# A convolution and a routed-attention block on one core: a lag of four steps, loads in smaller pieces, softmax sums by a shuffle, and the two halves of the TensorE array used for score products side by side

## The reference, cut to what matters

```python
q_reg, k_reg = qr.mean(2), kr.mean(2)
_, idx = jax.lax.top_k(jnp.einsum('brc,bsc->brs', q_reg, k_reg), TOPK)        # TOPK = 4, 49 regions
kg = take(kr, idx)     # 4 regions x 64 keys for each region's 64 queries
vg = take(vr, idx)
scores = jnp.einsum('brqhd,brkhd->brhqk', qh, kh) * scale                     # 8 heads, d = 8
attn = jax.nn.softmax(scores, axis=-1)
out = jnp.einsum('brhqk,brkhd->brqhd', attn, vh)
x = x + out @ wo + bo
x = x + gelu(layernorm(x) @ w1 + bm1) @ w2 + bm2
```

## Time and profile before

| | |
|---|---|
| median of 3 runs | 5555.56 us (5546.46 to 5559.63) |
| the profiled execution | 5569.85 us, span 5568.0 us |
| mean granted TensorE clock | 0.909 of full speed |
| TensorE busy | 4677.0 us, 84% of the span |
| VectorE, ScalarE, GpSimd busy | 62%, 59%, 49% |
| moved by the DMA queues | 487.33 MB, 88 GB/s on the mean |

### The profile page before, as it was taken

How to read it: one execution, slowest core, us unless ns; L and a number is a source line. 1 busy time by engine, 2 the same in 40 slices (tenths; PEclk the granted TensorE clock), 3 DMA queues, 4 the chain that set the end, 5 groups by cost and what they waited for, 6 DMA issues and landing times.

```text
span 5568.0 us, 230234 instructions
## 1 busy us (share of the span) xinstructions
PE 4677.0 (84%) x68754; PEld 3217.0 (58%) x68754; DVE 3447.6 (62%) x7969; ACT 3285.4 (59%) x6282; POOL 2747.0 (49%) x9656
## 2 busy tenths in 40 slices
PE   2388888888889888888888888888888888888888
PEld 1265565656556565565656656565565656556564
DVE  2266666666666666666666666666566666667665
ACT  1156556565665656556565665656556565665656
POOL 1245455454544545445454554545455454554553
PEclk8589999998998999889989999989899999989999
DMA  1333343333333333333333423333343333323311
GB/s 53 102 98 92 83 109 76 100 77 96 102 77 98 84 95 91 82 103 80 94 83 91 111 72 103 81 96 92 79 109 79 96 81 102 100 75 102 84 40 33
DMA packets 627124, 487.33 MB, mean 88 GB/s; under 512 B 483792, under 2 KB 613968, under 8 KB 615536
## 3 DMA queue, kind: packets, MB, share of 16 engines
q10 hardware_dynamic: 335360, 205.62, 16.4%
q1 hardware_dynamic: 290416, 265.73, 16.2%
HBM read 262.38 MB, written 208.73 MB: 85 GB/s over the span
## 4 chain that ended last, share of the span: by engine, by line
PE 45%; DMA 18%; issue 10%; SPq 7%; ACT 7%; DVE 5%; DVEq 3%; POOL 2%; ACTq 2%; POOLq 1%
DMA max_d<-tr 11%; PE ps L988 9%; PE ps L1002 7%; PE ps L1019 7%; PE ps L881 4%; DMA qm<-qk_d 3%; PE ps L938 3%; DMA xin<-in_x 3%; DVEq L223 2%; DVE mx L724 2%; SPq L327 2%; PE ps L949 2%; PE ps L901 2%; ACT hid L813 2%; PE ps L974 2%
## 5 line engine op out<-in xcount | busy, mean ns | idle before, releaser
L724 DVE TENSOR_REDUCE mx<-ps 128x4 f32<-128x1024 f32 x1568 | 1921.7, 1226 | 1702.3 <-PE ps L988 1354.0
L832 ACT ACTIVATE pt<-ps 128x512 f32<-128x512 f32 x3136 | 1694.3, 592 | 869.2 <-PE ps L1002 814.4
L506 POOL COPY vg<-vs 64x64 f32 x6272 | 1526.5, 243 | 782.0 <-POOL kg L490 576.7
L988 PE MATMUL ps<-kg,qm 96*128 96x256 f32 x6272 | 1336.2, 338 | 386.6 <-DVE mx L724 127.3
L490 POOL CAST kg<-ks 96x128 fp32r x3136 | 851.0, 297 | 1511.6 <-PE ps L1002 1156.6
L988 PEld LDWEIGHTS ps<-kg,qm 96*128 96x128 f32 x6272 | 946.8, 202 | 1053.6 <-issue 889.5
L1002 PE MATMUL ps<-qm,kg 97*128 97x256 f32 x6272 | 1119.8, 301 | 178.8 <-ACT pt L832 102.3
L1019 PE MATMUL ps<-pt,vg 128*32 128x64 f32 x50176 | 1091.4, 231 | 0.0
L1002 PEld LDWEIGHTS ps<-qm,kg 97*128 97x128 f32 x6272 | 926.2, 203 | 252.2 <-ACT pt L832 164.8
L1019 PEld LDWEIGHTS ps<-pt,vg 128*32 128x32 f32 x50176 | 826.1, 115 | 224.2 <-issue 34.8
L643 DVE CAST kg<-ks 96x128 fp32r x3136 | 625.6, 241 | 126.2 <-issue 123.5
(11 more groups left out here) (109 smaller groups left out, 3866.7 us busy)
## 6 DMA issues: line engine op xcount, KB each, us to landing
qk_d<-stg SPq DMA_DIRECT2D x224, 448.0 KB
qm<-qk_d ACTq DMA_DIRECT2D x1792, 42.0 KB
ks<-qk_d ACTq DMA_DIRECT2D x96, 784.0 KB, 6.2
vs<-v_d ACTq DMA_DIRECT2D x64, 784.0 KB, 6.7
xin<-in_x SPq DMA_DIRECT2D x119, 224.0 KB
xi_d<-xi SPq DMA_DIRECT2D x112, 224.0 KB
qk_d<-stg SPq DMA_DIRECT2D x112, 224.0 KB
max_d<-tr SPq DMA_DIRECT2D x1568, 2.0 KB
```

The lines of the kernel that those rows point to most:

```text
L506: j = pool.tensor_copy(dst.rearrange("p j (e x) -> p j e x", e=2)[:, :, :, 0:HD], vs[place(m)[0]][rows, bass.ds(region, 1), :].rearrange(" ...
L724: v.tensor_reduce(mx[h % 2][:].rearrange("p (g j e) -> p g j e", g=2, j=2)[:, :, :, 0], ps[:, 0:2, :].rearrange("p g (j k) -> p g j k", j= ...
L832: act.activation(pt[m % 2][:, c], ps[:, 2 + c, :], ACT.Exp, scale=float(HD) ** -0.5).then_inc(S["pt_ready"], 1)
L988: i = pe.matmul(ps[:, g, 256 * j:256 * j + 256], qm[c % 2][0:NP3, t, g, 2 * j:2 * j + 2, :].rearrange("p h t -> p (h t)"), kg[slot][0:NP3, ...
```

## The change

- **Lag.** `turned` and `attended` run four and five steps behind `scores`; the timetables of preparation, finish and routing shift by one step. SP issues the hop of step h first and then the row of step h-2. The rings `mx`, `tr`, `hopped` have 7 places, and the reduce waits for no hop.
- **Loads.** Keys and values of an image come in 20 transfers, spread over 23 steps (first image) and 34 steps (second), in place of 5 over 10. Queries go out as 4 and 4 transfers, in the steps with h mod 7 = 4 and 5. Input strips are worked every 7 steps, over 6 steps each.
- **Sums.** `pick` and its products (line 938) go; DVE spreads the sums by two shuffles of 128 x 448 per strip (`SPREAD`), and ACT takes the logarithm of that.
- **Halves.** Heads are held as pairs in the two halves of the partitions (rows 0 to 47 and 64 to 111, `NP3` = 48, the maximum in rows 48 and 112). `scores` makes four products of 48 rows by 128 by 256, two in each half of the array, each half into its own bank. `turned` makes eight products of 49 rows by 128 by 128 columns, four in each half; both banks are complete only at the end, and the first of them waits for both exponentials of the step before. The keys are kept with a row of -1 and copied over all 128 partitions.

```diff
-NP3 = 3 * HG * HD
+HALF = 64
+NP3 = 3 * 2 * HD
...
+SPREAD = [24] * HD + [25] * HD + [24] * 16
...
-ST_LAG = 3
-PV_LAG = 4
+ST_LAG = 4
+PV_LAG = 5
 AHEAD = 2
-LEAD = 18
+LEAD = 19
 END = STEPS + LEAD
-P_AT, P_EVERY = 18, 6
-F_AT, F_EVERY = 60, 7
-X_AT, X_EVERY = 62, 5
-ROUTE_AT = 62
+P_AT, P_EVERY = 19, 6
+F_AT, F_EVERY = 61, 7
+X_AT, X_EVERY = 62, 7
+ROUTE_AT = 63
 A_LOAD, B_LOAD = 70, 6
+A_SPAN, B_SPAN = 23, 34
 QK_DMAS, V_DMAS = 3, 4
-KV_DMAS = 5
+KV_DMAS = 20
...
-        pick = sb("pick", [128, 128])
...
-        qm = [sb(f"qm{i}", [128, NW, NG, HG, RT], F32R) for i in range(2)]
+        qm = [sb(f"qm{i}", [128, NW, NG, 2, RT], F32R) for i in range(2)]
...
-        mx = [sb(f"mx{i}", [128, 32]) for i in range(2)]
-        tr = [sb(f"tr{i}", [128, 32]) for i in range(2)]
+        mx = [sb(f"mx{i}", [128, 32]) for i in range(RING)]
+        tr = [sb(f"tr{i}", [128, 32]) for i in range(RING)]
...
-        hopped = [sem(f"hopped{i}") for i in range(2)]
+        hopped = [sem(f"hopped{i}") for i in range(RING)]
...
+                row = HALF * (h // 2) + 24 * (h % 2)
+                eng.dma_start(qm[c % 2][row:row + 24, :, g, h % 2, :].bitcast(F32), src[g, h]).then_inc(q_loaded[c % 2], 16)
...
+            if n < 12:
+                part, term, r0, r1 = n // 6, n // 2 % 3, R // 2 * (n % 2), (R // 2, R)[n % 2]
+                src = qk_d[bass.ds(q, 1), i, C:2 * C, term // 2, RT * r0:RT * r1].rearrange("o (g j c) n -> j (o c) g n", g=NG, j=2)[part]
+                dst = ks[i][HALF * part + term:HALF * part + NP3:3, :, r0:r1].rearrange("p g r t -> p g (r t)").bitcast(F32)
             else:
-                src = v_d[bass.ds(q, 1), i].rearrange("o t r n -> (o t) (r n)")
-                dst = vs[i][64 * (n - 3):64 * (n - 3) + 64].rearrange("p r n -> p (r n)")
+                half, r0, r1 = n % 2, (n - 12) // 2 * 12, ((n - 12) // 2 * 12 + 12) if n < 18 else R
+                src = v_d[bass.ds(q, 1), i, :, r0:r1, :].rearrange("o t r n -> (o t) (r n)")
+                dst = vs[i][64 * half:64 * half + 64, r0:r1].rearrange("p r n -> p (r n)")
...
+            if t in (ST_LAG, ST_LAG + 1) and live((c + 1) * NW, kind):
...
-                queries(eng, p + (c + 1) // 14, (c + 1) % 14, [(g, h) for g in range(NG) for h in range(HG)][(t - 3) * 3:(t - 2) * 3])
+                queries(eng, p + (c + 1) // 14, (c + 1) % 14, [(t - ST_LAG, h) for h in range(HG)])
...
-                if 0 <= h - A_LOAD < 2 * KV_DMAS and (h - A_LOAD) % 2 == 0:
-                    keys_values(eng, p + 1, 0, (h - A_LOAD) // 2)
-            local = h if kind == "lead" else h - STEPS
-            if local >= 0 and kind != "last":
+                for n in range(KV_DMAS):
+                    if h == A_LOAD + n * A_SPAN // KV_DMAS:
+                        keys_values(eng, p + 1, 0, n)
...
+                for n in range(KV_DMAS):
+                    if local == B_LOAD + n * B_SPAN // KV_DMAS:
+                        keys_values(eng, q, 1, n)
...
-                m = h - 1
-                if live(m, kind):
-
-                    sp.wait_ge(hopped[m % 2], (p * R + m // 2 + 1) * 16)
-                    settled(sp)
-                    sp.dma_start(qm[m // NW % 2][NP3:NP3 + 1, m % NW].rearrange("o g h t -> o (g h t)").bitcast(F32),
-                                 max_d[m % RING].rearrange("j p -> (j p)").unsqueeze(0)).then_inc(row_ready[m % RING], 16)
                 if live(h, kind):
                     sp.wait_ge(S["tr_ready"], T + 1)
                     settled(sp)
-                    sp.dma_start(max_d[h % RING].rearrange("j (b n) -> b j n", n=32), tr[h % 2][0:128:8, :]).then_inc(hopped[h % 2], 16)
+                    sp.dma_start(max_d[h % RING].rearrange("j (b n) -> b j n", n=32), tr[h % RING][0:128:8, :]).then_inc(hopped[h % RING], 16)
+                m = h - 2
+                if live(m, kind):
+
+                    sp.wait_ge(hopped[m % RING], (p * 14 + m // RING + 1) * 16)
+                    settled(sp)
+                    sp.dma_start(qm[m // NW % 2][NP3:128:HALF, m % NW].rearrange("o g e t -> o (g e t)").bitcast(F32),
+                                 max_d[m % RING].rearrange("(j g) p -> j (g p)", j=2)).then_inc(row_ready[m % RING], 16)
...
+                    if off in (0, 1):
+                        if off == 0:
+                            v.wait_ge(S["um_ready"], p * (4 * 14) + (NW + s + 1) * 4)
+                            settled(v)
+                        v.stream_shuffle(rc[:, off], um0[:, s] if off == 0 else um1[:, b], SPREAD).then_inc(S["sum_full"], 1)
...
-                    if live(h - 2, kind):
-                        v.wait_ge(hopped[h % 2], (p * R + (h - 2) // 2 + 1) * 16)
...
+                    if live(h - RING, kind):
+                        v.wait_ge(hopped[h % RING], (p * 14 + h // RING) * 16)
...
-                        act.activation(rc[:, i], ps[:, 5 + i, 0:ST], ACT.Ln).then_inc(S["lns_ready"], 1)
+                        act.activation(rc[:, i], rc[:, i], ACT.Ln).then_inc(S["lns_ready"], 1)
...
-                    if off == 0:
-                        pe.wait_ge(S["um_ready"], p * (4 * 14) + (NW + s + 1) * 4)
-                        if s >= 2:
-                            pe.wait_ge(S["ot_ready"], 1 + n - 1)
-                        elif kind == "loop":
-                            pe.wait_ge(S["l_ready"], (p + 2) * (2 * NW))
-                            pe.wait_ge(S["v_ready"], (p + 2) * NW)
-                        if s:
-                            pe.wait_ge(S["lnv2_ready"], n)
-                        for i, src in enumerate((um0[:, s], um1[:, s % 2])):
-                            pe.matmul(ps[:, 5 + i, 0:ST], pick[:], src, start=True, stop=True).then_inc(S["sum_full"], 1)
...
+                        elif kind == "loop":
+                            pe.wait_ge(S["l_ready"], (p + 2) * (2 * NW))
+                            pe.wait_ge(S["v_ready"], (p + 2) * NW)
...
-                        if s < NW - 1:
-                            pe.wait_ge(S["lns_ready"], n * 2 + 4)
+                        pe.wait_ge(S["ot_ready"], 1 + n)
+                        if s == 0 and kind == "loop":
+                            pe.wait_ge(S["lg_ready"], p + 2)
...
-                        i = pe.matmul(ps[:, g, 256 * j:256 * j + 256],
-                                      qm[c % 2][0:NP3, t, g, 2 * j:2 * j + 2, :].rearrange("p h t -> p (h t)"),
-                                      kg[slot][0:NP3, g].rearrange("p k t -> p (k t)"), start=True, stop=True)
+                        d = slice(HALF * j, HALF * j + NP3)
+                        i = pe.matmul(ps[:, j, 256 * g:256 * g + 256], qm[c % 2][d, t, g].rearrange("p e t -> p (e t)"),
+                                      kg[slot][d, g].rearrange("p k t -> p (k t)"), start=True, stop=True)
...
+                if not (isinstance(T, int) and T == 0):
+                    pe.wait_ge(S["pt_ready"], (T - 1) * 2 + 2)
                 for b in range(2):
-                    if not (isinstance(T, int) and T == 0):
-                        pe.wait_ge(S["pt_ready"], (T - 1) * 2 + b + 1)
                     for g in range(NG):
-                        i = pe.matmul(ps[:, 2 + b, 256 * g:256 * g + 256],
-                                      kg[slot][0:NP3 + 1, g, 2 * b:2 * b + 2, :].rearrange("p k t -> p (k t)"),
-                                      qm[c % 2][0:NP3 + 1, t, g].rearrange("p h t -> p (h t)"), start=True, stop=True)
-                    i.then_inc(S["st_full"], 1)
+                        for j in range(2):
+                            d = slice(HALF * j, HALF * j + NP3 + 1)
+                            n = 256 * b + 128 * g
+                            i = pe.matmul(ps[:, 2 + j, n:n + 128], kg[slot][d, g, 2 * b:2 * b + 2, :].rearrange("p k t -> p (k t)"),
+                                          qm[c % 2][d, t, g].rearrange("p e t -> p (e t)"), start=True, stop=True)
+                            if b == 1 and g == 1:
+                                i.then_inc(S["st_full"], 1)
```

59 lines of the change are left out of this document (23 added, 36 removed).

## The result

The changed kernel takes 6125.93 us (median of 4 runs, 6063.27 to 6144.33), the kernel before 5555.44 (5546.46 to 5559.63): the ratio is 1.101 [1.093, 1.109]. It is 10% slower; the forecast was 4960 us, within 4720 to 5380.

What follows compares the result with a forecast made beforehand. TensorE was taken to bound clean stretches, with 26 us a pair of excess. Terms -17 - 6.6 - 18 + 4 = -37.6 us a pair, x 16 = -602, +2, took 5556 to 4960 us, range 4720 to 5380.

Steps and rivals of the forecast that it cites:

- Queries and issues: +4 us: ScalarE's queue: four queries issued in one step make some of 14 blocks wait; +4 us a pair, 0 to 12.
- the signs: Expected changed profile: no reduce waiting for hops, row waits below 100 us, query waits below 250, clock above 0.93.
- The row is about even: Row issued after the maximum of step h+2, turned scores one step later: about even with before in short steps.
- Scores in halves -23.5 us: Scores on TensorE: four products cost two spacings, 0.24 us less a step, 23.5 us a pair where TensorE is the bound.
- clean finish cycle 20.8: Seven clean steps of finish take 20.8 us in place of 22.9, 2.1 less.
- -17 and -6.6: Savings a pair: 17 us from eight clean cycles of finish, 6.6 us from seven of preparation.
- ScalarE is the bound of finish: Rival: finish cycles stay at 22 to 22.9 us, filled by ScalarE's work, issues and lost overlap; about 5200 us, chance 0.13.
- Both rivals on rates: Short fp32r products need two passes, about 5600 us, chance 0.12; fp32r halves do not run together, 5900 us, 0.04.
- Lost overlap, half of 0.48: Turned scores wait for both exponentials: where ScalarE is late, overlap with the other bank's product, half of 0.48, is gone.
- Sums: -13.4 us of PE, shuffles covered: Dropping line 938 saves TensorE 13.4 us a pair; shuffles, 8.4 a pair, are covered by VectorE's slack in finish.
- Excess, 26 less 18: A pair takes 26 us beyond its clean cycles; lag, ring and spread loads remove 70%, 18 us (8 to 26).
- a clock that falls to its lower level because TensorE idles more often: Named last as something that would make the forecast wrong, beside short products at a lower rate; given no size or chance.

Runs made afterwards that it cites:

- e8: The changed kernel, halves kept, with queries issued in steps h mod 7 = 3 and 4 and the row one step earlier: 5655.07 us, ratio 1.016.
- e9: e6 with both exponentials awaited ahead of the first turned product and both banks released only at the end: 5551.42 us, ratio 1.000.
- e6: The changed kernel with scores and turned scores over the whole array, queries and row each issued one step earlier: 5396.93 us, ratio 0.971.
- e12: e6 with the sums on TensorE by the `pick` product again and `mx` in two places: 5335.62 us, ratio 0.961.
- e16: e8 with the sums on TensorE by the `pick` product again and `mx` in two places: 5543.97 us, ratio 0.995.
- e2: The kernel before with the halves alone added, its three key transfers becoming six: 5969.97 us, ratio 1.077.
- e4: The changed kernel with turned scores over the whole array again and only the scores in halves: 6082.09 us, ratio 1.096.
- e10: e6 with the scores alone in halves, turned scores over the whole array and waits as in e6: 5537.21 us, ratio 0.998.
- e13: e8 with three unneeded whole-array products of 384 columns ahead of the turned scores in three steps of seven: 5781.34 us, ratio 1.037.
- e11: e8 with one unneeded whole-array product of 512 columns ahead of the scores in each step: 5907.65 us, ratio 1.067.

## Why the prediction was wrong

From the changed kernel to the fastest one leads a chain of single edits, whose medians give 6125.93 - 233 (queries early) - 238 (row early) - 258 (halves undone, with their waits) - 61 (sums as product) = 5336. What is left of the change then (lag, ring, order of the hop) and the two moves (queries, row) give 220 us over the kernel before. The step that failed under all the terms is the clock. Savings and waits were priced as if it stayed up ("the clock above 0.93", TensorE busy near 4200 us); it was 0.765, with 2849 us at the lower level in place of 1013, and TensorE was busy for 4834.7 us. Of its terms, a pair:

- **"Queries and issues: +4 us" (0 to 12): mis-sized.** That blocks would wait was foreseen, even how long: 202.7 us came where the signs allowed 250, 104 waits in 16 pairs or about half of all blocks. The wait itself grew by (202.7 - 104.5) / 16 = 6.1 us a pair. But taking it away gave 233 / 16 = 15 in halves and 324 / 16 = 20 over the whole array. What was mis-sized is the price of a wait: the clock behind it was left out. The earlier trace rows showed how near it was: 3.0 us from issue to use for the first two, and 0.8 us later for the last of four.
- **"The row is about even".** The waits for rows grew from 73.8 to 164.9 us (forecast below 100), 5.7 a pair; taking them away gave 148 / 16 = 9 and 238 / 16 = 15. That the lag gives the turned scores one step more did not make up for the row being issued behind the maximum of two steps later.
- **"Scores in halves -23.5 us", "clean finish cycle 20.8", "-17 and -6.6": the local sum was right, what it does to a cycle was not.** The prediction took 0.64 us for the scores from the line of the turned ones; the scores' own line in the earlier trace rows has 0.72, and 0.50 came (forecast within 0.4), 0.22 less where 0.24 was forecast. Turned ones took 0.56 (within 0.65), six clean steps of preparation in e8 16.40 us (near 16.2). But in finish, with the clock full in both, halves shortened a cycle by 0.7 us (23.40 to 22.70). That is the time that the rival "ScalarE is the bound of finish" gave (22 to 22.9, chance 0.13), though ScalarE was busy for 17.05 us of it only, and TensorE for 18.18. And most cycles were not clean: the halves lost 104 us by themselves, +6.5 a pair, for a gain of some 24 that was forecast. Both rivals on rates fall: fp32r products of 128 columns cost no second pass.
- **"Lost overlap, half of 0.48": about right.** The forecast's cycle of 20.8 lies 1.5 above TensorE's sum of 19.3, 12 us a pair; the strict wait costs 10 a pair by itself (e9). ScalarE's exponential of one bank could run while TensorE wrote the other; now TensorE writes neither before both exponentials are done.
- **"Sums: -13.4 us of PE, shuffles covered".** The shuffle's 0.65 us were right (0.6). VectorE's slack did not cover them: with the shuffles the scores' wait for the maximum is 89 us longer (e6 against e12) and 93 (e8 against e16). Giving the sums back to TensorE made both e6 and e8 faster, by 4 and 7 us a pair.
- **Excess, 26 less 18.** The hop's wait did go. But the excess was read as the price of late hops alone. The kernel before spent 1013 us at the lower clock, and half of that, if TensorE is the bound throughout, is 32 us a pair, no less than the excess; the two overlap, and no run separates them. The spread loads were worth nothing; lag, ring and hop order, with queries and row put right, are worth 220 us, 14 a pair.

The forecast's last sentence, "a clock that falls to its lower level because TensorE idles more often", names what happened, and its price was in no range. The prediction had the numbers: the disturbed cycles of the earlier trace rows at clocks of 0.71 to 0.88 take 5 to 8 us more than the clean one. Counted in the clock's records, the kernel before has 142 stays at the lower level of 7.1 us on the mean, the changed one 286 of 9.9: the clock fell twice as often, as that sentence has it, and it also stayed down longer, which nothing in the prediction names. This should have been a rival with a chance of its own.

**What stays open.** That the halves lower the clock is measured (e9 to e8, e6 to e8, before to e2), with transfers out of play in the first two and the wait for the exponentials nearly so in the first (303.2 and 351.4 us). Through what: through idle time that the shorter products open ahead of ScalarE's exponentials, or through the work in halves itself? The stays at the lower clock, counted in the traces, speak for the second. e9 has 188 of them, 5.7 us on the mean; e8 212, of 10.8 us. So the halves add few falls, and nearly double each stay, although TensorE is busy for 87% of e9's and 89% of e8's. The same holds over all kernels: the stays are 7.9 to 10.8 us on the mean in the eight with turned scores in halves, and 5.7 to 7.3 in the ten with turned scores over the whole array, e4 and e10 with their scores in halves among them (7.3 and 6.5). The shortest of the first group is e13, which puts whole-array products ahead of the turned scores; e11, which puts one ahead of the scores, has 10.4. What in this work it is (49 rows, 128 columns, two at a time) no run separates, and so the cause of the longer stays is not shown.

## What to carry to other kernels

Where TensorE is the bound and its granted clock is not 1.00, price an edit twice: at full clock, and by whether it adds stops or gaps to TensorE, since behind stops like those above followed a stretch at half speed. When transfers are moved to a later step, compute for the last one of the burst the time from issue to use, and compare it with a landing read from the trace. Split a change of several parts before judging it: here the lag, the ring and the order of the hop, with a gain of 4%, were hidden below four parts with a loss of 14%. And where the array can be used in halves, put neighbouring products in the same shape: scores in halves beside turned scores that are not (e10) saved nothing at full clock.

## What the runs showed of the hardware

- Two products side by side, 48 rows in each half of the array, cost the time of one (four in 0.50 us, eight of 128 columns in 0.56), and fp32r products of 128 columns need no second pass. The Trainium skill (TensorEngine Tiling, section Tiling Modes, Key Properties) says that a change of tiling mode drains the engine; the trace agrees that a change has a price: with turned scores over the whole array behind scores in halves, turned scores start 0.43 us after scores in e10 where halves throughout (e8) have 0.34, and attended products 0.67 us after turned ones where e6 has 0.57. No run here measured the drain by itself.
- Halves lowered the mean granted clock from 0.909 (e6) to 0.883 (e10, scores alone), and with the strict wait from 0.903 (e9) to 0.798 (e8). In the second case the stays at the lower level became longer (5.7 to 10.8 us) rather than more frequent (188 to 212).
- One wait of 1.82 us was followed by 8.9 us at the lower clock (2395.80 to 2404.70 above).
- A shuffle of 128 x 448 fp32 takes 653 ns on VectorE, about as long as another operation of that size (610).
- Useless products did not pay in any of four places, though the clock rose from 0.765 to 0.828 in one.
